# Four-layer convolution network, second stage: one statistics chain per step, another way out of the first convolution's banks, seven banks in the ring

## The reference

```python
def _gn(v, G=8, eps=1e-5):
    g = v.reshape(B_, G, C_ // G, H_, W_)
    m = jnp.mean(g, axis=(2, 3, 4), keepdims=True)
    s = jnp.var(g, axis=(2, 3, 4), keepdims=True)
    return ((g - m) / jnp.sqrt(s + eps)).reshape(v.shape)
...
x = x + _L0_conv_ref(_gn(x), 5)                 # Newton-Schulz inverse of each 128 x 128 plane
x = x + _L1_conv_ref(_gn(x), weight_int8, scale_weight, bias)  # clip, round, 3x3, * scale + bias
x = x + _L2_conv_ref(_gn(x), filter_w)          # 5x5, the filter on the diagonal only
x = x + _L3_conv_ref(_gn(x), weight)            # circular 3x3, by FFT in the reference
```

## Time and profile before

| what | us |
|---|---|
| median of three runs | 3914.38 |
| the profiled execution's own time | 3911.49 |
| its span, first to last instruction | 3909.7 |
| PE matmul busy in the span | 3568.8 (91%) |
| DVE busy | 3149.0 (81%) |
| ACT busy | 2450.1 (63%) |
| POOL busy | 2419.3 (62%) |
| longest idle before a group: POOL L1223, behind ACT L1266 | 1064.9 |
| idle of DVE before L1321, behind PE L1453 | 237.9 |

### The profile page before, as it was taken

How to read it: one execution, slowest core, us unless ns; L and a number is a source line. 1 busy time by engine, 2 the same in 40 slices (tenths; PEclk the granted TensorE clock), 3 DMA queues, 4 the chain that set the end, 5 groups by cost and what they waited for, 6 DMA issues and landing times. The chain is left out here.

```text
span 3909.7 us, 137986 instructions
## 1 busy us (share of the span) xinstructions
PE 3568.8 (91%) x58569; PEld 2914.8 (75%) x58569; DVE 3149.0 (81%) x7205; ACT 2450.1 (63%) x4490; POOL 2419.3 (62%) x3156
## 2 busy tenths in 40 slices
PE   7999999999999999999999948888888888788888
PEld 7999999999999999999999924444444444444444
DVE  5888888888888888888888778888887878788774
ACT  5776777777777777777777635555555555555552
POOL 6888888888888888888888723333333333333332
PEclk9999999999999999999999968889899989998987
DMA  1221122212122212122121145555555555555552
GB/s 64 66 66 55 55 66 66 66 55 66 55 66 66 63 58 62 59 66 66 59 62 57 42 98 126 136 131 140 135 144 124 132 133 133 123 138 129 131 119 73
DMA packets 317732, 347.29 MB, mean 89 GB/s; under 512 B 21568, under 2 KB 284224, under 8 KB 300736
## 3 DMA queue, kind: packets, MB, share of 16 engines
q1 hardware_dynamic: 317120, 338.47, 33.6%
HBM read 135.09 MB, written 134.22 MB: 69 GB/s over the span
## 5 line engine op out<-in xcount | busy, mean ns | idle before, releaser
L1223 POOL TENSOR_TENSOR xn<-F,xn 128x512 f16<-128x512 f32 x512 | 542.0, 1091 | 1064.9 <-ACT xn L1266 1064.9
L1453 PE MATMUL bank<-xn,wt 64*32 64x512 bf16 (+1 forms) x18432 | 1062.2, 428 | 40.6 <-issue 27.1
L1453 PE MATMUL bank<-xn,wth 64*32 64x512 f16 (+1 forms) x6144 | 1044.9, 427 | 5.0 <-issue 4.7
L487 ACT ACTIVATE P<-bank 128x512 f32<-128x512 f32 x1024 | 606.0, 607 | 266.7 <-PE bank L1010 155.0
L1453 PEld LDWEIGHTS bank<-xn,wt 64*32 64x32 bf16 (+1 forms) x18432 | 460.7, 99 | 266.9 <-issue 129.9
L1321 DVE SCALAR_TENSOR_TENSOR x<-bank,wu,x 128x512 f32<-128x512 f32 x512 | 380.8, 744 | 237.9 <-PE bank L1453 236.2
L1453 PE MATMUL bank<-xk,wt 64*32 64x512 f16 x9216 | 530.7, 381 | 17.5 <-issue 17.2
L1453 PE MATMUL bank<-xk,wth 64*32 64x512 f16 x3072 | 522.1, 381 | 9.8 <-issue 9.8
L1453 PEld LDWEIGHTS bank<-xn,wth 64*32 64x32 f16 (+1 forms) x6144 | 396.3, 100 | 106.0 <-issue 9.7
L1263 ACT ACTIVATE F<-x,nb,r 128x2048 f32<-128x2048 f32 x128 | 268.5, 2097 | 275.2 <-DVE nb L1374 275.2
L337 POOL TENSOR_TENSOR W<-W 128x512 f16<-128x512 f32 x256 | 290.1, 1168 | 145.1 <-ACT W L520 145.1
(11 more groups left out here) (144 smaller groups left out, 8642.8 us busy)
## 6 DMA issues: line engine op xcount, KB each, us to landing
xk<-xn SPq DMA_DIRECT2D x1024, 65.9 KB, 2.4
X<-in_x SPq DMA_DIRECT2D x64, 1024.0 KB, 4.9
x_scratch<-X SPq DMA_DIRECT2D x64, 1024.0 KB, 5.6
X<-x_scratch SPq DMA_DIRECT2D x64, 1024.0 KB, 6.5
out<-x SPq DMA_DIRECT2D x64, 1024.0 KB, 4.5
wf<-in_w SPq DMA_DIRECT2D x2, 192.0 KB, 6.9
wf<-in_w SPq DMA_DIRECT2D x1, 320.0 KB, 7.3
whf<-in_w1h SPq DMA_DIRECT2D x6, 1.0 KB, 5.7
```

Of the source, the lines that this page charges most:

```text
L487: nc.scalar.activation(into[:, 4 * q:4 * q + 4, :], banks[q][:, :].rearrange("p (m w) -> p m w", m=4), ACT.Copy).then_inc(sb, 1)
L1223: ins = nc.gpsimd.tensor_tensor(padded(xn[l][n % 2], 1)[:, a + 1:a + 5, L:L + H], F[l][:, a:a + 4, :], padded(xn[l][n % 2], 0)[:, a + 1:a ...
L1453: ins = nc.tensor.matmul(bank[cols_, :], w, v, start=(half == i == 0), stop=(half == 1 and i == length[l] - 1))
```

## The change

Four edits, all in the second stage. (1) The banks of the first convolution are no longer evacuated by VectorE. ScalarE writes bank * scale + bias into x2 (`raise_`), and GpSimd adds X (`add`); `first` and the first-layer form of `residual` go. (2) The two chains of a step become one over two columns: x2 of image s-1 and x3 of image s-3. Its `mean` stands behind the pieces of the first convolution, its `var` behind the first piece of the third; the statistics of x2 so wait for the next step, and with them `upper`, `lower` and the skewed copies of layer 2, which move from step s to step s+1. `variance` goes to ScalarE, which takes the root with eps as its bias and writes var + eps beside it. `normalise` has two columns, so its per-partition scalars become tensors: four instructions with two SBUF inputs each. (3) One statistics bank is enough, and the ring has seven. (4) VectorE's order: chain, statistics of x2, `clamp` and `integers`, then all of layer 3, then layer 2.

```diff
-B_RING = 6
+B_RING = 7
...
+            def pair(s):
+                return there(s - 1) or there(s - LATE[2] - 1)
+            def stats_of(l, n):
+                return bst_[(n + 1 if l == 2 else n + LATE[2] + 1) % 2][:, l - 2, :, :]
...
 sync, after load(s + 2) and store(three):
-                        if there(s):
-                            need(sp, conv_ps[2], BPI * (s - 1))
-                            sp.wait_ge(high[2], s + 1)
-                            skew(s, 0)
-                            sp.wait_ge(normed[2], s + 1)
-                            skew(s, 1)
+                        if there(s - 1):
+                            need(sp, conv_ps[2], BPI * (s - 2))
+                            sp.wait_ge(high[2], s)
+                            skew(s - 1, 0)
+                            sp.wait_ge(normed[2], s)
+                            skew(s - 1, 1)
 gpsimd:
+                    def add(n, u):
+                        at = slice(4 * u, 4 * u + 4)
+                        pool.wait_ge(raised, BPI * n + u + 1)
+                        nc.gpsimd.tensor_tensor(xs_of(2, n)[:, at, :], xs_of(2, n)[:, at, :], xs_of(1, n)[:, at, :],
+                                                ALU.add).then_inc(evac[1], 1)
...
+                        if there(s):
+                            for u in range(BPI):
+                                add(s, u)
                         if there(mid):
                             lower(3, mid)
-                        if there(s):
-                            lower(2, s)
+                        if there(s - 1):
+                            lower(2, s - 1)
 scalar:
+                    def root(b):
+                        act.wait_ge(gvar, b + 1)
+                        nc.scalar.activation(cols["sd"][:, :], stat[:, 2:4], ACT.Sqrt, bias=epst[:, 0:1])
+                        nc.scalar.activation(cols["ve"][:, :], stat[:, 2:4], ACT.Identity,
+                                             bias=epst[:, 0:1]).then_inc(groot, 1)
+                    def raise_(n, u):
+                        if u == 0:
+                            need(act, evac[2], BPI * (n - 2))
+                        act.wait_ge(conv_ps[1], BPI * n + u + 1)
+                        nc.scalar.activation(xs_of(2, n)[:, 4 * u:4 * u + 4, :], bank_of(1, n, u)..., ACT.Identity,
+                                             scale=sws[:, 0:1], bias=bst[:, 0:1]).then_inc(raised, 1)
...
+                        if there(s):
+                            for u in range(BPI):
+                                raise_(s, u)
+                        if pair(s):
+                            root(s - 1)
                         if there(s + 1):
                             quotients(s + 1)
                         if there(mid):
-                            root(3, mid)
-                            upper(3, mid)
-                        if there(s + 1):
-                            first(s + 1)
-                        if there(s):
-                            root(2, s)
-                            upper(2, s)
+                            upper(3, mid, s - 1)
+                        if there(s - 1):
+                            upper(2, s - 1, s - 1)
 vector:
+                        link.done(nc.vector.tensor_tensor(c["rb"][:, :], c["ra"][:, :], c["ra"][:, :], ALU.mult))
+                        link.done(nc.vector.tensor_tensor(c["rb"][:, :], c["rb"][:, :], c["ve"][:, :], ALU.mult))
...
+                        if pair(s):
+                            whole_stats(s - 1)
+                            deviations(s - 1)
                         for u in range(BPI):
                             if there(s):
-                                residual(1, s, u)
                                 chunk_stats(2, s, u)
+                            if u == 1 and pair(s):
+                                normalise(s - 1)
                         if there(s + 1):
                             clamp(s + 1)
                             integers(s + 1)
-                        for u in range(BPI):
-                            if there(three):
+                        if there(three):
+                            for u in range(BPI):
                                 residual(3, three, u)
-                        for u in range(BPI):
-                            if there(two):
+                        if there(two):
+                            for u in range(BPI):
                                 residual(2, two, u)
                                 chunk_stats(3, two, u)
 tensor:
-                            pe.wait_ge(evac[m], BPI * i + v + 1)
+                            pe.wait_ge(raised if m == 1 else evac[m], BPI * i + v + 1)
...
-                        if there(mid):
-                            mean(3, mid)
+                        if pair(s):
+                            if there(two - 1):
+                                finish(2, two - 1, BPI - 1)
+                            mean(s - 1)
                         for u in range(BPI):
                             if there(three):
                                 piece(3, three, u)
-                            if there(mid) and u == 0:
-                                var(3, mid)
-                            if there(s) and u == 1:
-                                mean(2, s)
+                            if u == 0 and pair(s):
+                                var(s - 1)
                         for u in range(BPI):
                             if there(two):
                                 piece(2, two, u)
-                            if there(s) and u == 0:
-                                var(2, s)
```

More of the change, by code:

```diff
@@ L1145, in conv_net @@
             evac = [None] + [sem(f"evac{l}") for l in (1, 2, 3)]
[L1146 to L1153, removed]
+            bst_done = sem("bst_done")
+            gmean = sem("gmean")
+            spread = sem("spread")
+            gvar = sem("gvar")
+            gvar_sb = sem("gvar_sb")
+            groot = sem("groot")
+            gchain = sem("gchain")
+            CH = 9
             GAP = BEHIND = 2
@@ L1315, in residual @@
                         dve.wait_ge(conv_ps[l], BPI * n + u + 1)
-                        if l == 1 and u == 0:
-                            dve.wait_ge(biased, n + 1)
                         if l == 2 and u == 0:
                             need(dve, out_stored[n % THIRD], 16 * (n // THIRD))
-                        col = sws if l == 1 else wtop[l]["u"]
-                        nc.vector.scalar_tensor_tensor(out=dst, in0=bank, scalar=col[:, 0:1], in1=xs_of(l, n)[:, at, :],
+                        nc.vector.scalar_tensor_tensor(out=dst, in0=bank, scalar=wtop[l]["u"][:, 0:1], in1=xs_of(l, n)[:, at, :],
@@ new lines, in pieces, with whole_stats, deviations @@
+                    def pieces(b, k):
+                        return bst_[(b + 1) % 2][:, :, :, :].rearrange("p l u (a e) -> p l (u a) e", e=3)[:, :, :, k]
+                    def whole_stats(b):
+                        for l, n in ((2, b), (3, b - LATE[2])):
+                            dve.wait_ge(gathered[l], BPI * max(0, min(n + 1, B)))
+                        nc.vector.tensor_reduce(cols["s"][:, :], pieces(b, 1), AX.X, ALU.add).then_inc(bst_done, 1)
+                    def deviations(b):
+                        link = Link(dve, gchain, CH * b)
+                        dve.wait_ge(gmean, b + 1)
+                        link.done(nc.vector.tensor_tensor(dev[:, :, :], pieces(b, 1),
+                                                          stat[:, 0:2].unsqueeze(2).broadcast_to([H, 2, 2 * BPI]),
+                                                          ALU.subtract))
+                        link.done(nc.vector.tensor_copy(cols["m"][:, :], stat[:, 0:2]))
@@ L1499, in _ @@
                         two, mid, three = images_of(s)
-                        for u in range(BPI):
-                            if there(s):
+                        if there(s):
+                            for u in range(BPI):
                                 piece(1, s, u)
-                        if there(mid):
-                            mean(3, mid)
+                            if not there(two):
+                                finish(1, s, BPI - 1)
+                        if pair(s):
+                            if there(two - 1):
+                                finish(2, two - 1, BPI - 1)
+                            mean(s - 1)
                         for u in range(BPI):
@@ L1507, in _ @@
                                 piece(3, three, u)
-                            if there(mid) and u == 0:
-                                if there(s):
-                                    finish(1, s, BPI - 2)
-                                var(3, mid)
-                            if there(s) and u == 1:
-                                mean(2, s)
+                            if u == 0 and pair(s):
+                                var(s - 1)
+                        if there(three) and not there(two):
```

(5 more changed lines are left out.)

121 lines of the change are left out of this document (42 added, 79 removed).

## The result

The changed kernel takes 3719.76 us (median of three runs, 3712.07 to 3722.94) against 3914.38: ratio 0.9504, 95% interval 0.9476 to 0.9532. The forecast was 3596, range 3540 to 3720. The direction was right; of the 318 us forecast, 195 came. Two later timings of the same kernel gave 0.9496 and 0.9488.

What follows compares the result with a forecast made beforehand. VectorE's order was taken as directly costing PE 3.9 us a step, lower clock 2.25. Steps from 24.49 to 19.3 over 59 give 306 us, tail 12; 3911.5 becomes 3593.5, plus 2.9 for the median: 3596, range 3540 to 3720.

Steps and rivals of the forecast that it cites:

- what PE does by itself: 17.63 us, the floor of a step: Second stage: PE's own work in a changed step at full clock, summed from traced pieces without waits, 17.63 us.
- 19.3 for the 18.8: Changed step: 18.76 us walked, range 18.76 to 20.8, taken as 19.3 because hops between four engines were not all included.
- the reading of rows 2: Two neighbouring steps before, 22.24 us at clock 0.99 and 25.54 at 0.81: 22.24 structure, 2.25 lower clock on the mean.
- The step that I rebuilt: Old step from trace rows: waits of 1.52 and 2.40, mean, var and PE's pieces, together 22.24 us.
- The var's wait gone, the mean's left at 1.1 to 1.7: PE's stops before the small matmuls: var's 2.40 us go, mean's 1.52 becomes 1.1 to 1.7 us.
- the clock rival: The remaining stop leaves the mean clock cost of 2.25 us a step: steps 21.55, total 3735 us; chance 0.15.
- VectorE blocked by GpSimd: Two-input VectorE instructions stand until the GpSimd sum beside them ends; `normalise` ends at 6.5 instead of 5.05 us.
- The slower rival: VectorE stands behind GpSimd again and again, 10.6 us on its loop: steps 28.1 us, total 4137; chance 0.05.
- The copies: Second layer's skewed copies, now in the step of their use: land at 27.3, wanted at 27.9, slack 0.6 us.
- That rival: The skewed copies take the bound, 1.8 us a step on 19.0: steps 20.8, total 3687 us; chance 0.16.
- the seventh bank: Bank ring of the second stage: the seventh bank removes nothing, as no wait of PE for a bank was seen.
- Tail and filling: Ends of the second stage: tail gains 12 us (bounds 0 and 20), pipeline filling 0 (bounds -10 to +10).

Runs made afterwards that it cites:

- half: Changed kernel with two 64 x 64 matmuls a strip instead of four 64 x 32, edge row shift left out, half of PE's code: 3615 us, ratio 0.9248.
- wide: Changed kernel with one 64 x 128 matmul a strip instead of four 64 x 32, edge row shift left out: 3627 us, ratio 0.9238.
- no_adds: Changed kernel with GpSimd's sum of x1 replaced by a one-element memset, so x2 lacks x1: 3708 us, ratio 0.9452.
- dve_evac: Changed kernel with the first edit undone: VectorE evacuates the first layer with the sum, ScalarE adds the bias beforehand: 3723 us, ratio 0.9506.
- act_evac: Kernel before with the first edit alone: ScalarE and GpSimd evacuate the first layer, two chains and six banks stay: 4096 us, ratio 1.0454.
- bias_late: Changed kernel with the first edit undone and ScalarE's bias moved behind upper of layer 2: 3730 us, ratio 0.9542.
- m64: Changed kernel with three matmuls a strip in layers 1 and 3, one of them 64 wide, row shift kept: 5228 us, ratio 1.336.

## Why the prediction was wrong, step by step

**The step that failed** is the term "what PE does by itself: 17.63 us, the floor of a step", taken with full clock and no more stops than the mean's. The 17.63 come out again as a remainder. From the table: 21.28 less 1.04, 0.09 and 1.85 of stops, less 21.28 x 0.031 = 0.66 for the clock, leaves 17.64. What was missing are 1.85 us of stops behind PE's code and the 0.66 of clock, 2.5 us; 0.5 of it was covered by having taken 19.3 for the 18.8 worked out. At 59 steps the other 1.96 us are 116 of the 124 us that failed to come; the rest is nearly all the filling. The agreement at 17.6 is partly luck. The same remainder is 17.0 in half and 16.8 in wide, so some 0.6 us or more of it goes with the code stops too; each stop costs more than its recorded idle time, as the one above shows, and the rest is open. Against that the wait for the mean is 0.5 us longer without code stops. What the code costs in all is 1.9 us a step, 21.28 less 19.37.

**Where it began** is the reading of rows 2. I took 22.24 us as the structure and put the 2.25 us up to the mean on the clock alone. The mean step of before is 3.12 of waits, 2.40 of clock (24.45 x 0.098), 0.94 of code stops and 17.99 of work. The step that I rebuilt had no code stop in it; 25 of the 59 have none, and PE waits 3.6 us in them on the mean, against 2.9 in the others. Nor did its slower neighbour in rows 2 have the same waits, as the prediction says: 2.9 us in the second window, 4.2 in the first. The page of before had the sign, in the idle time of this row:

```profile
L1453 PE MATMUL bank<-xn,wt 64*32 64x512 bf16 (+1 forms) x18432 | 1062.2, 428 | 40.6 <-issue 27.1
```

**The change's balance,** before to after: waits for the small matmuls -2.08, clock -1.74, PE's own work -0.35, copies +0.09, code +0.91; together -3.17. The clock terms count whole steps; by the clock's record 0.24 us of before's falls into waits, where it costs nothing, so that work and clock share their 2.1 us a little otherwise. The forecast had the mechanism of the first four terms; the fifth, a stop that other waits had hidden, was not among its rivals.

**The var's wait gone, the mean's left at 1.1 to 1.7:** right, 0 and 1.04 (1.6 in the forms without code stops).

**The clock:** its rival fell, 0.97 against 0.90. It is not 1.00, and the wide forms, with the mean's stop alone, have 0.93. Why those two differ is open.

**VectorE blocked by GpSimd:** right in kind and size, 0.43 and 1.20 us at the median against 0.16 without the sums, but not the bound: no_adds and dve_evac bring nothing. The slower rival fell. The sum took ScalarE's evacuation at 0.6 us; it measures 0.777, to no effect on the step.

**The copies:** slack of about 0.6 us was right to the point that they bind as soon as anything moves them by 2 us (dve_evac), and worth 0.35 us a step at most here. That rival's 3687 us is 33 off. Nearest to the result lay the clock rival, 3735 us and steps of 21.55 against 21.26, by another cause: it kept 2.25 us a step for a low clock, and measured are 0.66 of clock and 1.85 of code stops.

**Costed at nothing:** the seventh bank, rightly. **Tail and filling:** -11 and +10 against -12 and 0.

**Shown and not shown.** Shown: the stops end 2.1 to 3.0 us behind the start of a code load, and vanish with half the code. Also that they grow where other waits shrink, and partly fill what those leave: in act_evac, before, dve_evac, changed and bias_late the waits for small matmuls and copies are 6.8, 3.1, 1.85, 1.1 and 1.1 us, and the code stops 0.1, 0.9, 1.0, 1.85 and 2.0. All nine forms with the full code and one chain lie between 20.9 and 21.7 us a step. Open: why the loads come so unevenly, and whether the order of PE's work could place them better. One load in three has a stop behind it. One in four starts more than 160 matmuls after its forerunner, where 126 are the mean; behind these lie three quarters of the stopped time. Other DMA traffic is at most a small part: a load with a stop behind it took no longer (0.98 us) than one without (1.10).

The Trainium skill ("Runtime: NRT & Kernel Launch", Instruction fetch mechanics) says that code is fetched in 16 KiB blocks of 256 instructions and that crossing a block is mostly hidden. The block size agrees with the trace: 576 matmuls and as many weight loads a step are 4.5 blocks, and 4.56 loads are seen. "Mostly hidden" does not: 1.85 us of 21.28 are not.

## What to carry to other kernels

When the bound is an engine whose unrolled code is tens of KB a step, take the "issue" stops of its waits as a term of their own before forecasting a full gain: removed waits can come back in part as code stops until the code shrinks. To rebuild a mean step, average over many; the tidiest one has left out just what will bind next. And an edit that moves work to another engine is priced by what stands ahead of it in that engine's queue: the same four sums were free behind a `lower` that was done in time, and cost 4.5% behind one that waited for this step's late chain.

## What the hardware showed unexpectedly

- PE's stops behind its code: resumed mostly 2.25 to 2.45 us after the start of a 16 KB load, 1.3 us long at the median and 2.6 at most, none with 2.29 loads in a step of 19.4 us.
- Column tiles of 32 and 64 in turn: 0.67 us for a pair of strips against 0.22 with equal tiles (m64).
- A VectorE instruction with two SBUF inputs waited for the GpSimd sum beside it, 1.20 us where 0.16 is its own time.
- ScalarE took 777 ns for 128 x 512 out of a bank with a scale and a bias column (L1306), where L487 in the earlier trace rows took 597.
